# Feed-forward of an attention-convolution hybrid: the next norm as a side stream on off-diagonal tiles, and one copy on VectorE in place of ScalarE

## What is computed

```python
x = window_attention_block(x)   # shifted 7x7 windows, 3 heads, layer norm, MLP with gelu, residuals
x = conv_block(x)               # x + silu(conv3x3(layernorm(x) @ w_in))
t = tokens(x)                   # 3136 tokens of 24 channels per image
t = t + spectral_mixer(layernorm(t))      # relu, FFT over tokens, relu, inverse FFT, linear (layer 2)
t = t + quantized_ffn(layernorm(t))       # layer 2
t = t + spectral_mixer(layernorm(t))      # layer 3
t = t + quantized_ffn(layernorm(t))       # layer 3

def quantized_ffn(x, W1, b1, W2, b2):     # 24 -> 96 -> 24
    h = relu(fp16(fp16(fp8(x) @ fp8(W1)) + fp8(b1)))
    return fp16(fp16(fp8(h) @ fp8(W2)) + fp8(b2))
```

## Time and profile before

| | |
|---|---|
| median of three runs | 3321.04 us |
| the profiled execution | 3324.36 us |
| its span, first to last instruction | 3322.6 us |
| TensorE matmul busy | 2898.2 us (87%) |
| VectorE busy | 1665.9 us (50%) |
| ScalarE busy | 1611.3 us (48%) |
| GpSimd busy | 363.6 us (11%) |
| mean granted TensorE clock | 0.971 |
| chain of work that ended last | TensorE 69%, ScalarE 13%, VectorE 7%, issue 7%, SyncE's queue 3% |

### The profile page before, as it was taken

How to read it: one execution, slowest core, us unless ns; L and a number is a source line. 1 busy time by engine, 2 the same in 40 slices (tenths; PEclk the granted TensorE clock), 3 DMA queues, 4 the chain that set the end, 5 groups by cost and what they waited for, 6 DMA issues and landing times.

```text
span 3322.6 us, 110007 instructions
## 1 busy us (share of the span) xinstructions
PE 2898.2 (87%) x49148; PEld 1838.1 (55%) x49148; DVE 1665.9 (50%) x2707; ACT 1611.3 (48%) x2899; POOL 363.6 (11%) x574
## 2 busy tenths in 40 slices
PE   6868889888899898998989989888898988988888
PEld 3536546466455573564744747447465474553754
DVE  5524546355553545544464445644457354572554
ACT  3542455533555425644266353563535535456245
POOL 4520010000100011001010011000110001100001
PEclk8989999999999999999999999999999999999999
DMA  2322000210001100110001100021000210001100
GB/s 80 69 59 52 2 16 5 53 33 2 17 16 50 25 2 17 32 51 6 2 18 42 46 1 2 18 54 34 1 2 19 54 34 1 2 19 34 33 1 16
DMA packets 28434, 84.79 MB, mean 26 GB/s; under 512 B 22002, under 2 KB 23138, under 8 KB 24114
## 3 DMA queue, kind: packets, MB, share of 16 engines
q1 hardware_dynamic: 26690, 72.55, 9.1%
q0 software_dynamic: 1280, 5.21, 0.6%
HBM read 61.70 MB, written 14.84 MB: 23 GB/s over the span
## 4 chain that ended last, share of the span: by engine, by line
PE 69%; ACT 13%; DVE 7%; issue 7%; SPq 3%; DMA 1%; ACTq 0%; DVEq 0%
PE ps L1128 69%; ACT lv L719 2%; SPq L495 2%; ACT area_ty L851 2%; ACT rs L724 2%; ACT sq L707 1%; DMA area_hz<-f_all 1%; DVE xs L1098 1%; DVE area_hz L979 1%; ACT area_hz L762 1%; ACT sq L705 1%; ACT area_ty L843 1%; DVE area_hz L996 1%; DVE area_ty L1094 1%; DVE area_ty L1070 1%
## 5 line engine op out<-in xcount | busy, mean ns | idle before, releaser
L1128 PE MATMUL ps<-area_hz 32*49 32x147 f32 (+3 forms) x7180 | 363.7, 288 | 89.2 <-DVE area_hz L979 24.1
L1128 PE MATMUL ps<-area_ty,area_hz 113*64 113x49 f32 (+2 forms) x10240 | 409.5, 256 | 8.8 <-ACT area_ty L741 8.1
L827 ACT ACTIVATE area_hz<-ps 121x384 f32<-121x384 f32 (+2 forms) x256 | 129.6, 519 | 583.5 <-PE ps L1128 583.5
L1128 PE MATMUL ps<-sq,keep_sb 64*64 64x392 f32 (+1 forms) x1728 | 340.2, 540 | 68.5 <-ACT sq L707 44.7
L1128 PEld LDWEIGHTS ps<-area_hz 32*49 32x49 f32 (+3 forms) x7180 | 290.2, 151 | 183.4 <-issue 160.9
L1128 PEld LDWEIGHTS ps<-area_ty,area_hz 113*64 113x64 f32 (+2 forms) x10240 | 319.4, 132 | 82.1 <-issue 80.9
L1128 PE MATMUL ps<-area_ty,g_sb 56*112 56x192 f32 (+1 forms) x3712 | 311.5, 321 | 26.0 <-DVE area_ty L1070 19.7
L1128 PEld LDWEIGHTS ps<-area_ty,g_sb 56*112 56x112 f32 x3712 | 293.0, 173 | 44.7 <-issue 44.0
L1128 PE MATMUL ps<-xs,keep_sb 64*64 64x448 f32 (+1 forms) x1184 | 217.2, 543 | 80.4 <-DVE xs L1098 49.7
L1070 DVE COPY area_ty<-ps 120x896 f32<-120x896 f32 (+1 forms) x192 | 164.8, 858 | 236.9 <-PE ps L1128 236.9
L719 ACT ACTIVATE lv<-ps 128x448 f32<-128x448 f32 (+1 forms) x304 | 158.6, 522 | 220.3 <-PE ps L1128 220.3
(11 more groups left out here) (124 smaller groups left out, 4325.7 us busy)
## 6 DMA issues: line engine op xcount, KB each, us to landing
area_hz<-f_all SPq DMA_DIRECT2D x16, 2541.0 KB
xw<-x_in SPq DMA_DIRECT2D x8, 1568.0 KB, 6.8
y_out<-xs SPq DMA_DIRECT2D x32, 252.0 KB
f_all<-piece POOLq DMA_DIRECT2D x16, 317.6 KB, 3.7
area_hz<-raw_in SPq DMA_DIRECT2D x1, 2894.0 KB, 9.4
g_sb<-g_in SPq DMA_DIRECT2D x6, 355.2 KB
area_ty<-area_hz SPq DMA_DIRECT2D x128, 9.2 KB
g_sb<-g_in SPq DMA_DIRECT2D x2, 710.5 KB
```

Source lines behind the costliest of these rows:

```text
L827: act.activation(dst, src, ACT.Relu if st in (ST_H, ST_F2) else ACT.Copy).then_inc(sc_kept, 1)
L1128: return pe.matmul(o, a, b, start=start, stop=stop)
```

## The change

The next norm of the feed-forward gets semaphores, buffers and a PSUM bank of its own (bank 3 for both its centering and its variance; `side_sq`, `side_lv`, `side_rs`), and its matmuls go onto the off-diagonal quadrants, issued in pairs with those of the feed-forward's own norm (`together`), or alone (`crossed`) where there is none. Its scaling multiplies the activations themselves, in SBUF, in place of the centered values in PSUM; the centering is folded into the weights of queries, keys and values at the start (for the mixer it already was). The lag in l = 0 grows from two slots to three, the slots from ten to eleven. The copy of the down product moves from ScalarE to VectorE. The orders within a slot change on all three engines. One `keep_busy` of the window MLP goes.

```diff
-FFN_SLOTS = NT + 3
+SIDE_LAG = 3
+FFN_SLOTS = NT + SIDE_LAG + 1
+        side_sq, at = part(area_y, 0, TT)      # and side_lv, side_rs
@@ center_bank(k): {LN_MIX(1): 1, LN_WIN1: 1}.get(which, 0)  ->  i % 2
@@ variance_bank(k): {LN_MIX(1): 3, LN_WIN1: 3}.get(which, 2)  ->  2
@@ ScalarE, ffn
+                    if 0 <= s - 1 < NT:
+                        log(q, LN_FFN(l), s - 1)
+                    if done:
+                        log_side(q, *done)
+                    if 0 <= s - 1 < NT:
+                        inverse_root(q, LN_FFN(l), s - 1)
+                    if done:
+                        root_side(q, *done)
+                    if s < NT:
+                        square(q, LN_FFN(l), s)
+                    if new:
+                        square_side(q, *new)
-                        act.activation(o16[:, s % 2, :], ps[:, 7, 0:TT], ACT.Copy
-                                       ).then_inc(f_out, 1)
...
@@ VectorE
+            def scale_side(q, which, i):
+                w = ln_width(which)
+                ve.wait_ge(side_root, side_count(q, which, i))
+                o, a, b = xh[:, w * i:w * i + w], xw[:, w * i:w * i + w], side_rs[:, 0:w]
+                if which == LN_MIX(1):
+                    o = xhc[:, :, TR * i:TR * i + TR].rearrange("p w h -> p h w")
+                    a, b = (v.rearrange("p (h w) -> p h w", w=HW) for v in (xs[:, w * i:w * i + w], b))
+                ve.tensor_tensor(o, a, b, ALU.mult).then_inc(side_normed, 1)
@@ VectorE, ffn
+                    done = side_tile(l, s - 1 - (0 if l else SIDE_LAG))
+                    if done:
+                        scale_side(q, *done)
+                    if 0 <= s - 2 < NT:
+                        k = l * NT + s - 2
+                        ve.wait_ge(f_down, q * 2 * NT + k + 1)
+                        ve.tensor_copy(o16[:, s % 2, :], ps[:, 7, 0:TT]).then_inc(f_out, 1)
...
+            su(ve.tensor_copy(wq[:, :], ps[:, 0, 384:512]))      # and wk, wv: centered weights
@@ TensorE, setup
+                mm(ps[:, 0, 384:512], K("center"), wq[:, :]).then_inc(su_pe, 1)      # and wk, wv
+            pe.wait_ge(su_ve, N_SETUP_VE + 6)                    # ahead of first_keys(0)
@@ TensorE, mlp
                         if i == 1:
-                            keep_busy(4, 1)
@@ TensorE, ffn
+                        along = (variance_bank(k), TT, K("variance"), sq[:, k % 2, 0:TT])
+                        if done:
+                            made, side = together(along, across)
+                            side.then_inc(side_var_made, 1)
...
+                    if new:
+                        if l == 0:
+                            pe.wait_ge(ffn_added, q * 2 * NT + new[1] + 1)
...
+                        if new[1] >= 1:
+                            pe.wait_ge(side_logged, side_count(q, *new) - 1)
+                        w, x = ln_width(new[0]), xw if l else xs
+                        across = (3, w, K("center"), x[:, w * new[1]:w * new[1] + w])
+                    if s < NT:
+                        k = LN_AT[LN_FFN(l), s]
+                        pe.wait_ge(ve_kept, q * VE_FILLS + vector_fills(step_of(l, ST_FFN, s) + 1))
...
+                        along = (center_bank(k), TT, K("center"), xs[:, TT * s:TT * s + TT])
+                        if new:
+                            made, side = together(along, across)
+                            side.then_inc(side_centered, 1)
...
-                    if l == 0 and s > NT:
+                    if l == 0 and NT < s < FFN_SLOTS - 1:
                         keep_busy(4, 1)
```

More of the change, by code:

```diff
@@ L118, in _tile_order @@
                 order.append((LN_FFN(l), s))
[L119 to L122, removed]
     return order
@@ L134, in ln_count, with side_count, side_tile @@
     return q * LN_N + NW + k + 1
+SIDE_N = NT + NW
+def side_count(q, which, i):
+    return q * SIDE_N + (i if which == LN_MIX(1) else NT + i) + 1
+def side_tile(l, i):
+    if l == 0:
+        return (LN_MIX(1), i) if 0 <= i < NT else None
+    return (LN_WIN1, i) if 0 <= i < NW else None
 def ln_width(which):
@@ L157, in center_bank @@
     assert not in_pairs(which)
-    return {LN_MIX(1): 1, LN_WIN1: 1}.get(which, 0)
+    return i % 2
 def variance_bank(k):
@@ L167, in variance_bank @@
         return 6
-    return {LN_MIX(1): 3, LN_WIN1: 3}.get(which, 2)
+    return 2
 def user_before(bank, k):
@@ L708, in square, with log @@
                                ).then_inc(squared, 1)
-            def invert(q, which, i):
+            def log(q, which, i):
                 k = LN_AT[which, i]
@@ L720, in invert, with inverse_root @@
                                    ).then_inc(logged, 1)
+            def inverse_root(q, which, i):
+                k = LN_AT[which, i]
+                w = PT if in_pairs(which) else ln_width(which)
                 if two_before(k):
@@ L830, in ffn @@
             def ffn(q, l):
+                lag = 0 if l else SIDE_LAG
                 for s in range(FFN_SLOTS):
+                    done, new = side_tile(l, s - 1 - lag), side_tile(l, s - lag)
                     if 0 <= s - 1 < NT:
[L833 to L842, removed]
-                        act.activation(o16[:, s % 2, :], ps[:, 7, 0:TT], ACT.Copy
-                                       ).then_inc(f_out, 1)
+                        log(q, LN_FFN(l), s - 1)
[9 more added lines that the diff above has]
+                        square_side(q, *new)
                     if 0 <= s - 1 < NT:
@@ L1586, in ffn @@
             def ffn(q, l):
+                lag = 0 if l else SIDE_LAG
                 for s in range(FFN_SLOTS):
+                    done, new = side_tile(l, s - 1 - lag), side_tile(l, s - lag)
+                    if done:
+                        pe.wait_ge(side_squared, side_count(q, *done))
+                        across = (3, ln_width(done[0]), K("variance"), side_sq[:, 0:ln_width(done[0])])
                     if 0 <= s - 1 < NT:
-                        variance(q, LN_FFN(l), s - 1)
+                        k = LN_AT[LN_FFN(l), s - 1]
+                        pe.wait_ge(squared, ln_count(q, k))
+                        before = user_before(variance_bank, k)
+                        if before is not None:
+                            pe.wait_ge(logged, ln_count(q, before))
+                        along = (variance_bank(k), TT, K("variance"), sq[:, k % 2, 0:TT])
+                        if done:
+                            made, side = together(along, across)
+                            side.then_inc(side_var_made, 1)
+                        else:
+                            made = blocks(*along)
+                        made.then_inc(var_made, 1)
+                    elif done:
+                        crossed(*across).then_inc(side_var_made, 1)
                     if s < NT:
```

86 lines of the change are left out of this document (50 added, 36 removed).

## The result

| | before | changed |
|---|---|---|
| median (four runs each, same chip) | 3323.91 us (3319.8 to 3327.95) | 3238.59 us (3226.67 to 3250.57) |
| ratio, 95% interval | | 0.9743 [0.9703, 0.9783] |
| the profiled execution, its span | 3324.36, 3322.6 us | 3226.67, 3225.0 us |
| mean granted TensorE clock in it | 0.971 | 0.969 |

The account below looks back on a forecast made before the run. TensorE was taken as nearest its limit. Per quad -5.8 - 4.3 - 0.8 + 0.2 = -10.7, eight quads -85.6, with -7.5 and +2.1 -91.0: 3233.4 us profiled, 3230 us median, range 3203 to 3266.

Parts of the forecast that it names:

- The steady slots: Feed-forward slots 2 to 6: TensorE's and VectorE's loops meet at 4.98 us a slot; l = 0 -5.8, l = 1 -4.3 us.
- centering to down product: Term of TensorE's slot loop: from the centering until the down product starts, 1.07 us, including 0.01 for the second pair.
- the hidden tile's loop: Loop from down product through copy, relus and GpSimd's conversion to the next down product: 4.79 us, below the 4.98 us slot.
- The price of a second pair: TensorE's side passes on the other two quadrants add 0.01 us a pair; bounds 0.01 to 0.75 to 0.9.
- Rival 2: Pairs with 448 columns don't overlap on TensorE, each costing 0.75 us more: 3340 us, slower; chance 0.04.
- Rival 1: VectorE's side scale collides with GpSimd's conversion and lengthens it by 0.93 or 0.55 us: 35 us, 3265 us; chance 0.11.
- The ends: From slot 6's residual add to the end of each feed-forward: l = 0 -0.8 us, l = 1 +0.2 us a quad.
- The prediction's own sign of being wrong on the ends: Wrong on the ends if TensorE waits for bank 3, the side bank, longer than 0.6 us.
- The removed keep_busy: Window MLP: the centering after the removed matmul starts about 0.94 us sooner, 8 times, -7.5 us; bounds 0 and -8.7.
- The start: Program start: first keys wait for six setup copies, moving from 43.67 to 45.8, +2.1 us once.
- The median: Whole kernel: 3233.4 us for the profiled execution, the median 3.3 us lower, so 3230 us.
- rival 3: The new 0.82 us gap in each slot lowers TensorE's clock to 1.2 GHz: +4.2 us in 64 slots, 3500; chance 0.02.

Follow-up runs that it names:

- experiment 8: Changed kernel without two implied waits in front of TensorE's centering pair (one in l = 1, both in steady l = 0 slots): 3220.9 us, ratio 0.9706.
- experiment 3: Changed kernel with VectorE's side scale moved behind the copy of the down product: 3268.3 us, ratio 0.983.
- experiment 4: Changed kernel with the side tile's matmuls on the same diagonal quadrants as the feed-forward's own, one pair after the other: 3333.75 us, ratio 1.0026.
- Experiment 2: Changed kernel with the down product's copy back on ScalarE, behind the squares: 3229.31 us, ratio 0.9721.
- Experiment 7: Changed kernel without the keep_busy matmuls in slots 8 and 9 of l = 0: 3225.7 us, ratio 0.9712.
- experiments 1: The changed kernel once more, nothing edited, beside runs of the kernel before: 3237.27 us, ratio 0.9737.
- experiment 10: The changed kernel a third time, unedited, on the chip of the kernel with both trims: 3243.05 us, ratio 0.9744.

## Why the prediction was right, and where it was off

**The steady slots: right, each loop as forecast.** Predicted 4.98 us, measured 4.87 in l = 1. One term was mis-sized: centering to down product, taken as 1.07, is 0.90. I had read 0.97 as the pitch of a 392-column piece, but before, the down product that followed waited for the residual add (866.42 + 0.68 = 867.10, product at 867.25); the pitch of the 448-column piece in front of the mixer's product, 0.90, was the row to take. The handover back came out at 0.11 for 0.07 and the products at 1.24 for 1.22: 4.98 - 0.17 + 0.06 = 4.87. In l = 0 the handover is 0.26 instead of 0.07, the cost of the added waits in TensorE's queue, which I had put at nothing; that makes 5.04, and experiment 8 gets 0.11 of it back. That the row of l = 0 in the table comes within 1.2 us of its forecast is in part luck: in the last two of its four slots the two errors, -0.17 and +0.19, cancel, and in the first two (4.81 and 4.88) the side stream is only starting. VectorE's copy was 0.62 as taken, and the hidden tile's loop 4.80 by experiment 3.

**The price of a second pair: right**, 0.98 us with 448 columns, and experiment 4 gives the other side: 0.65 (392 columns) to 0.74 us (448) more for each pair without the off-diagonal quadrants, 0.75 forecast, and no gain left. Rival 2 would have been that kernel: 3340 forecast for it, 3333.75 measured.

The Trainium skill's page "TensorEngine Tiling (Array Packing)", section "Restrictions and Gotchas", says that different row tiles cannot access the same PSUM bank at once, by which a pair would cost its full price; with 0.98 against 0.97 us this kernel's trace disagrees, for these f32 passes.

**Rival 1 (collision): half right.** The side scale and the conversion do collide, but it is VectorE that waits and not GpSimd, so the time forecast for it, 3265, didn't come. In the slots of l = 1 they overlap by 0.32 us and the side scale takes 0.74 instead of 0.56; in the last slot by 1.25, and it takes 1.67. With 448 columns it is 1.06 instead of 0.93 for 0.26 us and 1.93 for 1.15. Experiment 2 adds 1.34 (392) for 0.92 and 1.61 (448) for 0.82. In all six the lengthening is the overlap less 0.14 us or so, so the instruction stands still until shortly before the conversion ends; an overlap of 0.12 us, in experiment 4, costs nothing (0.56). In all of them the conversion had begun first; the other order does not occur.

The Trainium skill's page "SBUF — State Buffer", section "Who interferes with whom", describes such an exclusive lock between VectorE with two SBUF inputs and a GpSimd instruction that reads SBUF; these traces agree: 1.67 us for 0.56 when the conversion has 1.25 us left. From the rule I had the side scale wait until 1.5 and end at 2.45 us after the add; it ended at 2.29 (727.66 to 729.95), ahead of the copy at 2.64.

**The ends: right at full clock.** l = 0 -0.8 a quad: 20.46 to 19.68 in the five quads where both kernels have full clock; the other three were 1.4 to 1.6 us longer before, at the lower clock, which is why the sum is -10.5 for -6.6. l = 1: 15.21 for 15.3 forecast. The prediction's own sign of being wrong on the ends did come: TensorE is idle for 0.73 us in front of the last side centering, where more than 0.6 was to count against it. Experiment 7 shows 0.65 of it to be the bank's (the centering at +13.86 instead of +14.51), so the wait was seen rightly and mis-sized by 0.05.

**The removed keep_busy: right for a quad at like clock, less in sum.** At like clock a quad gives 0.95 to 1.1 us, 0.94 forecast. Net it is 5.6 us between the two profiled executions and 5.0 to 7.7 over the others, since the lower clock that the matmul had sat out falls in part on the centering. The prediction had no term for that.

**The start: +3.2 for +2.1.** The first keys are 3.0 us later. Timeline of the changed kernel:

```profile
44.23 0.46 DVE L1159 COPY wconv<-ps 128x288 f32<-128x288 f32 x1 [0.46 <-PE ps L1179]
46.26 0.26 DVE L1164 COPY wv<-ps 128x96 f32<-128x96 f32 x1
46.67 0.51 PE L1179 MATMUL ps<-area_ty,wk 64*64 64x392 f32 x1 [2.47 <-DVE wv L1164]
```

The three added copies cost what I gave them (45.61 to 46.52), but the first copy now also waits for the three added products (`su_pe` 12 in place of 9) and starts at 44.23 instead of 43.44. That wait I had not counted.

**The median: the sum was of the profiled execution, and that was a lucky one.** Forecast 3233.4 for it, measured 3226.7; but I took the median to lie 3.3 us below, and it lay 12 above. In the 13 runs of the changed kernel (first result, experiments 1 and 10) time goes with the mean granted clock, correlation -0.95, about 24 us for 0.01. Their mean clock is 0.964, that of 29 runs of the kernel before 0.970. So the change does lose clock, some 14 us by that slope (an estimate), though not where rival 3 put it: none of its three profiles has a low-clock microsecond in slots 2 to 6. Lower-clock time is 196 us in the profile of the kernel before and 200, 222 and 253 in the three of the changed one. It grew in three places above all: in the stretch of the removed keep_busy (31 us before, 47, 37 and 58 after), in the end of l = 1 (5 before, 15 to 17 after), and in the first slots of l = 1, where the profile of the kernel before has none: 7, 17 and 31 us in one, two and three quads, each such quad 2.8 to 3.9 us longer. The end of l = 0 and the second mixer together have less (40 before, 3 to 10 after). Windows of the third profile, experiment 10:

```profile
820.00:826.00 6.00, 6.00 (x130) 6.00 (x128) 2.37 (x5) 2.17 (x4) 1.39 (x9) 1.00 0.01 3
826.00:832.00 6.00, 3.71 (x38) 1.29 (x34) 1.49 (x3) 1.14 (x3) 0.00 (x0) 0.82 0.00 0
832.00:838.00 6.00, 4.76 (x24) 0.84 (x24) 1.69 (x3) 2.15 (x5) 0.00 (x0) 0.50 0.00 0
```

TensorE leaves the mixer fully busy and is busy 3.71 of the next 6 us, and then runs at the 1.2 GHz level. Why this quad and not its neighbour, which does the same work, no run settles. Filling these slots was not tried.

## What to carry to other kernels

When TensorE's matmuls use only two quadrants, look for a second stream of the same shape before reordering: here no gain was left without the pairs (96 us), and one engine's part of the new order alone cost 57 us, because an instruction placed early waits for one that its supplier still issues late. Whether the pairs would have gained as much in the old order was not tried. Take a pitch from rows where nothing waits, count every wait in the queue in front of the instruction that closes the loop, and ask which products a shared count waits for. And give the sum for the profiled execution a spread for the clock before calling it a median.

## What the hardware showed that I had not expected

- Satisfied waits at the head of TensorE's queue need not be free: two of four gone took the handover of l = 0 from 0.26 to 0.15 us, 2.3 us in sum over the eight quads; one of three gone in l = 1 took it from 0.11 to 0.15.
- When VectorE's two-input SBUF product starts during GpSimd's conversion, only the product pays, by their overlap less some 0.14 us; the conversion is 1.31 us with the collision and without.
- The same kernel has its low-clock stretches in other quads at every execution, 200 to 253 us in sum in its three profiles; over 13 runs its time goes from 3223 us at a mean clock of 0.970 to 3251 at 0.959.
- The fill matmuls in the end of l = 0 were not what held the clock there: without them it stayed at 1.00, and 7 us were gained.
